# Attention stage of a four-stage block on one core: value bias as a one-row product, value eviction and query normalisation on ScalarE, normalisation statistics in other slots

## Chip, cores and metric

The kernel runs on one core of a Trainium2 chip. The metric is the device time of one execution in microseconds (us), from the first to the last instruction and what lies around them; lower is better. TensorE (PE) does matrix products and transposes, VectorE (DVE), ScalarE (ACT) and GpSimd (POOL) work element by element, SyncE (SP) issues the transfers.

## What is computed

The input x is 16 batches of 128 rows by 256 columns. Four residual parts follow one another: a recurrent mixing part, a gated feed-forward part, a cross attention and a mixture of experts. Only the cross attention and the last quarter of the feed-forward part, which runs beside its first batches, matter here:

```python
x = x + tanh(g_xattn[0]) * wkv(layernorm(x), ctx)
x = x + tanh(g_ffn[0])   * gated_ffn(layernorm(x))
x = x + tanh(g_xattn[1]) * attention(target=layernorm(x), source=ctx)   # 16 heads of 8
x = x + tanh(g_ffn[1])   * moe(layernorm(x))

# attention, for each batch:
q = Wq @ target + bq ;  k = Wk @ source + bk ;  v = Wv @ source + bv    # 128x256 each
amap = softmax(mask * (q.T @ k) / sqrt(8) - (1 - mask) * 1e6) * mask     # 256x256 per head
out  = amap @ v
```

layernorm(x) is (x - mean) / sqrt(var + 1e-5) over the 256 columns.

## The kernel before, in words

All four parts are written out by hand: each engine has its own list of instructions, and semaphores (names a_..., s_...) order them across engines. An engine works its list off strictly in order, so a wait holds up all that stands behind it.

The attention is a software pipeline over 16 batches. One batch is eight slots p = 0 to 7; batch b = 4g + k, with k the place in its group of four. The loop `turns` writes out group 0 (b = 0 to 3), runs groups 1 and 2 (b = 4 to 11) as a hardware loop and writes out the last group and one batch more. What is done in the eight slots of batch b belongs to several batches:

- the maxima of the scores of batch b+2. TensorE writes 16 score tiles (L782, 128x512 each as two products of 256 columns) by turns into two PSUM banks, and VectorE reduces each to row maxima (`dve_reduce`, L907). Two tiles, two reduces in each slot. I call these reduces R0 to R15. Score tile n+2 waits until reduce n has read its bank (`score_bank`, L796).
- the exponentials of batch b. TensorE writes the turned scores (L787) between the score products (`pe_both`), ScalarE takes the exponential of 128x1024 (`act_exp`, L982), and TensorE multiplies by the values (`pe_pv`, L853, two slots later).
- values of batch b+3: in slot 6 `pe_v` (L767) multiplies the context by Wv into the bank MISC, two products of 128x128. In slot 7, between R14 and R15, VectorE adds the bias row (bvb, a copy in all 128 partitions) and writes VF (`dve_vf`, L899). GpSimd makes VP of it (L1012).
- queries and keys of batch b+4. Statistics of x in slot 0 on VectorE, between the reduces (`dve_stats`, L876, L880, L883), the power -1/2 on GpSimd (`power_step`, L145), and in slot 1, between R2 and R3, VectorE writes the normalised tile Z3 (`dve_z3`, L893). TensorE makes the keys (L759) and then the queries (L763) of it in slot 1. ScalarE evicts both (`act_qk`, L958); masking, splitting and a trip through memory follow.
- the end of batch b-1: transposes on TensorE (L862 in slot 3, L869 in slot 5), the division and the addition to x on VectorE (L918 to L943).

One bank, MISC, holds by turns the values, the maxima turned (L841), keys and queries, and both transposes; each user waits until the one before has been evicted.

Ahead of slot 0 there is a prologue. The last quarter of the feed-forward part runs there on TensorE (L395, L431), and the projections and values of batches 0 to 2 stand between its products. VectorE does the feed-forward's element work (L409, L417), z3 and vf of these batches, and the reduces of batches 0 and 1.

## Time and profile before

| what | us |
|---|---|
| median of three runs | 611.96 |
| lowest and highest of them | 610.57, 614.04 |
| the profiled execution | 612.62 |
| span of that execution, first to last instruction | 610.9 |
| from one value product to the next, batches 1 to 11 | 14.39 |

The rows further down come from the profiled execution. "busy" is the time in which an engine works on an instruction; `[0.46 <-DVE MX L907]` behind a row says that the engine sat idle for 0.46 us before it and what ended that. A timeline row merges like instructions that follow each other: its first number is the start of the first one, its second the time until the end of the last. The end of a product lies later than the start of the next, since TensorE overlaps them, so on TensorE distances between starts are what counts. A product of 32-bit numbers shows as two MATMUL records, one for each of two passes; "x4" at L767 is therefore two products. The tile size ahead of the shape (60\*128, 64\*128, 128\*128, 128\*32) is the number of rows and columns of the array that the product uses.

### The profile page before, as it was taken

What the parts mean: (1) busy time and instruction counts of PE and PEld (TensorE: products, weight loads), DVE (VectorE), ACT (ScalarE), POOL (GpSimd) and SP (SyncE); (2) the same over time, 40 slices, a digit from 0 to 9 for tenths busy, and PEclk for the clock granted to TensorE, in tenths of its full rate; (3) what the DMA queues carried; (4) which work ended last, traced back from release to release, by engine and by line L of the source; (5) the groups of instructions that cost most, each with busy time, mean ns of one, the idle gap of its engine ahead of it and who ended that gap; (6) DMA issues with size and microseconds to landing.
All of it is one profiled execution on the core that took longest, in us unless ns stands there. A gap on an engine that the chain in (4) does not pass through costs nothing. (4 is left out here: it accounts for less than half of the span.)

```text
span 610.9 us, 10613 instructions
## 1 busy us (share of the span) xinstructions
PE 508.4 (83%) x3368; PEld 269.3 (44%) x3368; DVE 407.8 (67%) x881; ACT 228.1 (37%) x330; POOL 205.7 (34%) x350
## 2 busy tenths in 40 slices
PE   1159899999798879999999998989879999899960
PEld 1034554644453433333333433333333555788850
DVE  4978678687535778888888888886946333333224
ACT  1003012031032027777777777767611010132310
POOL 2514115132265134554545545531210710022220
PEclk9999999999999969999999999999979999999995
DMA  6602006673228334555555555530040220266518
GB/s 165 213 1 69 1 0 134 88 188 141 58 70 224 87 93 134 154 148 148 149 138 140 137 136 153 140 83 7 3 141 2 103 69 0 66 187 190 185 40 275
DMA packets 70882, 68.11 MB, mean 111 GB/s; under 512 B 9136, under 2 KB 63328, under 8 KB 70848
## 3 DMA queue, kind: packets, MB, share of 16 engines
q1 hardware_dynamic: 69312, 63.48, 38.9%
q0 software_dynamic: 1536, 4.20, 1.9%
q8 instruction: 18, 0.29, 0.2%
q14 instruction: 16, 0.13, 0.1%
HBM read 41.04 MB, written 26.62 MB: 111 GB/s over the span
## 5 line engine op out<-in xcount | busy, mean ns | idle before, releaser
L907 DVE TENSOR_REDUCE MX<-psum 128x2 f32<-128x512 f32 x256 | 166.7, 682 | 32.0 <-PE psum L782 32.0
L982 ACT ACTIVATE HP<-psum 128x1024 f32<-128x1024 f32 x128 | 129.9, 1023 | 56.5 <-PE psum L787 54.6
L782 PE MATMUL psum<-QKA 60*128 60x256 bf16 x512 | 86.3, 279 | 21.0 <-DVE MX L907 19.4
L395 PE MATMUL psum<-space_a,space_w 128*128 128x512 f32 (+1 forms) x192 | 89.8, 616 | 5.0 <-ACT space_a L384 2.9
L787 PE MATMUL psum<-QKA 60*128 60x256 bf16 x512 | 84.9, 276 | 0.2 <-ACT HP L982 0.2
L853 PE MATMUL psum<-HP,VP 128*32 128x256 f32 x1024 | 81.8, 393 | 0.3 <-issue 0.2
L782 PEld LDWEIGHTS psum<-QKA 60*128 60x128 bf16 x512 | 33.5, 95 | 82.0 <-DVE MX L907 68.1
L395 PEld LDWEIGHTS psum<-space_a,space_w 128*128 128x128 f32 (+1 forms) x192 | 34.4, 187 | 49.1 <-issue 39.1
L431 PE MATMUL psum<-space_w,HP 128*128 128x256 f32 x192 | 50.8, 402 | 2.2 <-DVE HP L417 2.2
L1629 PE MATMUL psum<-space_a,wsh 128*128 (+3 forms) x96 | 45.2, 622 | 1.1 <-PEq L1120 1.1
L1703 PE MATMUL psum<-XT,WE 128*128 128x256 f32 (+1 forms) x192 | 44.1, 380 | 1.6 <-ACT XT L1584 1.6
L1557 POOL DMA_INDIRECT combined<-OE,to_u x16 | 15.3, 959 | 87.4 <-ACT OE L1597 85.0
L431 PEld LDWEIGHTS psum<-space_w,HP 128*128 128x128 f32 x192 | 33.9, 193 | 16.5 <-issue 12.4
L1703 PEld LDWEIGHTS psum<-XT,WE 128*128 128x128 f32 (+1 forms) x192 | 34.2, 181 | 8.2 <-issue 1.1
L403 ACT ACTIVATE space_a<-psum,hgs 128x512 f32<-128x512 f32 (+1 forms) x24 | 16.5, 686 | 56.5 <-PE psum L395 56.5
L1012 POOL TENSOR_TENSOR VP<-VF,maskT 128x32 f32<-128x32 f32 x128 | 25.9, 239 | 28.0 <-DVE VF L899 14.8
L145 POOL TENSOR_TENSOR rstd<-veps,neghalf 128x1 f32<-128x1 f32 (+1 forms) x21 | 15.7, 748 | 54.5 <-DVE veps L127 44.4
L787 PEld LDWEIGHTS psum<-QKA 60*128 60x128 bf16 x512 | 31.1, 95 | 6.1 <-issue 2.9
L994 POOL TENSOR_TENSOR QK<-QK,MB 128x512 f32<-128x512 f32 x16 | 20.3, 1268 | 40.0 <-ACT QK L958 40.0
L409 DVE SCALAR_TENSOR_TENSOR space_a<-space_a,psum 128x512 f32<-128x512 f32 (+1 forms) x24 | 16.1, 672 | 24.1 <-ACT space_a L403 24.1
L853 PEld LDWEIGHTS psum<-HP,VP 128*32 128x32 f32 x1024 | 20.4, 108 | 26.5 <-issue 22.0
L1837 DVE SCALAR_TENSOR_TENSOR H1s<-THs,psum 128x256 f32<-128x256 f32 (+1 forms) x24 | 10.1, 420 | 28.8 <-ACT THs L1591 27.8
(167 smaller groups left out, 710.3 us busy)
## 6 DMA issues: line engine op xcount, KB each, us to landing
QKA<-stack_scr SPq DMA_DIRECT2D x32, 480.0 KB, 5.3
stack_scr<-PARTS SPq DMA_DIRECT2D x32, 192.0 KB, 2.1
WE<-in_W SPq DMA_DIRECT2D x16, 352.0 KB
stack_scr<-PARTS SPq DMA_DIRECT2D x32, 128.0 KB, 1.9
dispatched<-zeros SPq DMA_DIRECT2D x8, 257.0 KB, 3.6
XD<-dispatched SPq DMA_DIRECT2D x8, 257.0 KB, 3.0
X<-in_x SPq DMA_DIRECT2D x4, 512.0 KB, 3.6
CV<-in_ctx SPq DMA_DIRECT2D x4, 512.0 KB, 4.6
```

The source lines that it names most:

```text
L395: last = pe.matmul(bank[2 * (i % 2) + side][0:m, :], (gw, uw)[side][:, h, i * P:i * P + m], ZT[:, h, :], start=(h == 0), stop=(h == 1))
L403: act.activation(TH[0:m, i % 2, :], bank[2 * (i % 2)][0:m, :], ACT.Tanh, scale=hgs[0:m, i:i + 1]).then_inc(s_th, 1)
L431: last = pe.matmul(DB[t // 2][:, (t % 2) * C:(t % 2 + 1) * C], HP[0:m, i, t * P:(t + 1) * P], dw[0:m, i, :], start=(i == 0), stop=(i == NI ...
L782: return pe.matmul(SBK[n % 2][:, tt * T:(tt + 1) * T], QKA[rows, k, 0, h, tt * P:(tt + 1) * P], QKA[rows, k, 1, h, :], start=True, stop=True)
L787: return pe.matmul(TBK[st][:, j * T:(j + 1) * T], QKA[rows, k, 1, h, st * P:(st + 1) * P], QKA[rows, k, 0, h, :], start=True, stop=True)
L853: last = pe.matmul(PVB[32 * j:32 * j + 32, grp * T:(grp + 1) * T], VP[:, k, st, 4 * j + i, :], PT[:, i % 2, st, j, :], start=(i in (0, 3) ...
L907: dve.tensor_reduce(MX[:, par, head_of(n), :], SBK[n % 2][:, :].rearrange("p (a s) -> p a s", a=2), axis=AX.X, op=ALU.max).then_inc(a_red, 1)
L982: act.activation(PT[:, i % 2, st, :, :].rearrange("p j t -> p (j t)"), TBK[st], ACT.Exp)\
L994: pool.tensor_tensor(QK2, QK2, MB[:, k, :].unsqueeze(1).broadcast_to([P, 2, T]), ALU.mult).then_inc(a_masked, 1)
L1012: last = pool.tensor_tensor(dst, src, maskT[:, st, bass.ds(b, 1)].unsqueeze(2) .broadcast_to([P, 4, 8]), ALU.mult)
L1629: last = pe.matmul(bank[2 * i + side][0:m, :], (wsh1, wsh3)[side][:, h, i * P:i * P + m], ZT4[:, h, bass.ds(GT * g, GT)], start=(h == 0), ...
L1703: last = pe.matmul(bank[i][0:m, lo:lo + CAP], w[:, s, h, i * P:i * P + m], XT[:, s, h, :], start=(h == 0), stop=(h == 1))
```

## The change

1. Values: `pe_v` adds to each of its two products a second one that accumulates onto it: a stationary row of 128 ones (`one_row`, one partition) times one row of bvb. The eviction, now without an addition, moves to ScalarE (`act_vf`): in slot 7 behind the exponential.
2. Normalised query tile: ScalarE computes it as Identity(rstd * x + shift) (`act_z3`), with shift = -mean * rstd. VectorE makes negm = -mean beside veps (`dve_shift_terms`), GpSimd multiplies by rstd behind the power (`pool_shift`).
3. Other slots: for a batch at place 0 of its group, statistics and power stay in slot 0 of the batch four before it, and z3 stands in slot 1, ahead of that slot's exponential. For places 1 to 3 the statistics go to slots 5 and 6, the power and the shift to slot 6 and z3 to slot 7 of the batch five before it, so a whole slot 0 lies between z3 and the query product.
4. Prologue: z3 and vf of its batches stand in ScalarE's list.

```diff
@@ pe_v
                     for st in range(2):
-                        last = pe.matmul(MISC[:, st * P:(st + 1) * P], CX[:, k, st * P:(st + 1) * P], wv[:],
-                                         start=True, stop=True)
+                        pe.matmul(MISC[:, st * P:(st + 1) * P], CX[:, k, st * P:(st + 1) * P], wv[:], start=True, stop=False)
+                        last = pe.matmul(MISC[:, st * P:(st + 1) * P], one_row[:, :], bvb[0:1, :], start=False, stop=True)
                     last.then_inc(a_vps, 1)
@@
-                        dve.tensor_scalar(veps[:, 0:1], mv[:, 0:1, 1], EPS, None, ALU.add).then_inc(a_var, 1)
-
+                        dve_shift_terms(dve, 1)
+
+                def dve_shift_terms(dve, n):
+
+                    dve.tensor_scalar(veps[:, 0:n], mv[:, 0:n, 1], EPS, None, ALU.add).then_inc(a_var, 1)
+                    dve.tensor_scalar(negm[:, 0:n], mv[:, 0:n, 0], -1.0, None, ALU.mult).then_inc(a_var, 1)
@@
-                def dve_z3(dve, b):
+                def pool_shift(pool, n, nth):
+
+                    pool.wait_ge(a_var, 2 * nth)
+                    if later(nth - 1):
+                        pool.wait_ge(a_z3, nth + 2)
+                    pool.tensor_tensor(rstd[:, 0:n], veps[:, 0:n], neghalf[:, 0:n], ALU.pow).then_inc(a_rstd, 1)
+                    pool.wait_ge(a_rstd, nth)
+                    pool.tensor_tensor(shift[:, 0:n], negm[:, 0:n], rstd[:, 0:n], ALU.mult).then_inc(a_shift, 1)
+
+                def act_z3(act, b):
                     n = b if isinstance(b, int) and b < GB else 0
-                    dve.wait_ge(a_rstd, LN_COUNT(b))
+                    act.wait_ge(a_shift, LN_COUNT(b))
                     if later(b):
-                        dve.wait_ge(a_proj, b)
-                    dve.tensor_scalar(Z3[:], xb(b), mv[:, n, 0:1], rstd[:, n:n + 1], ALU.subtract, ALU.mult).then_inc(a_z3, 1)
-
-                def dve_vf(dve, b):
-                    dve.wait_ge(a_vps, b + 1)
+                        act.wait_ge(a_proj, b)
+                    act.activation(Z3[:], xb(b), ACT.Identity, bias=shift[:, n:n + 1], scale=rstd[:, n:n + 1]).then_inc(a_z3, 1)
+
+                def act_vf(act, b):
+                    act.wait_ge(a_vps, b + 1)
                     if later(b):
-                        dve.wait_ge(a_vp, b)
-                    dve.tensor_tensor(VF[:, :, :], MISC[:, 0:T].rearrange("p (s c) -> p s c", s=2),
-                                      bvb[:, :].unsqueeze(1).broadcast_to([P, 2, P]), ALU.add).then_inc(a_vf, 1)
+                        act.wait_ge(a_vp, b)
+                    act.activation(VF[:, :, :].rearrange("p s c -> p (s c)"), MISC[:, 0:T], ACT.Copy).then_inc(a_vf, 1)
@@ ScalarE's slot
+                            if p == 1 and k == 0 and there(b, AHEAD_Q):
+                                act_z3(act, b + AHEAD_Q)
...
+                            if p == 7 and there(b, AHEAD_V):
+                                act_vf(act, b + AHEAD_V)
+                            if p == 7 and k < GB - 1 and there(b, AHEAD_LN):
+                                act_z3(act, b + AHEAD_LN)
@@ GpSimd's slot
-                            if p == 0 and there(b, AHEAD_Q):
-                                power_step(pool, 1, a_var, a_rstd, LN_COUNT(b + AHEAD_Q))
+                            if p == 0 and k == 0 and there(b, AHEAD_Q):
+                                pool_shift(pool, 1, LN_COUNT(b + AHEAD_Q))
+                            if p == 6 and k < GB - 1 and there(b, AHEAD_LN):
+                                pool_shift(pool, 1, LN_COUNT(b + AHEAD_LN))
```

How this stands in the lists of the engines, first on TensorE. In slot 6 of a batch of the first group, the value products stand between the last attention product of the slot (L853) and the first score product of slot 7. Before:

```order
L787 MATMUL psum<-QKA 128x256
L853 MATMUL psum<-HP,VP 32x256 x4
L767 MATMUL psum<-wv,CX 128x128 x2
L782 MATMUL psum<-QKA 128x256
L787 MATMUL psum<-QKA 128x256
```

and in the changed kernel:

```order
L792 MATMUL psum<-QKA 128x256
L858 MATMUL psum<-HP,VP 32x256 x4
L772 MATMUL psum<-wv,CX 128x128
L773 MATMUL psum<-bvb,one_row 128x128
L772 MATMUL psum<-wv,CX 128x128
L773 MATMUL psum<-bvb,one_row 128x128
L787 MATMUL psum<-QKA 128x256
```

Two products have become four, and full ones (128 rows of the array) alternate with one-row ones.

VectorE from slot 5 of one batch to slot 3 of the next, in the first group (MX are the reduces, X<-X,psum is the addition of the batch before in slot 5). Before:

```order
L943 TENSOR_TENSOR X<-X,psum 128x256
L907 TENSOR_REDUCE MX<-psum 128x2 x3
L899 TENSOR_TENSOR VF<-psum,bvb 128x256
L907 TENSOR_REDUCE MX<-psum 128x2
L876 BN_STATS stats<-X 128x6
L907 TENSOR_REDUCE MX<-psum 128x2
L880 BN_AGGR mv<-stats 128x2
L907 TENSOR_REDUCE MX<-psum 128x2
L883 TENSOR_SCALAR veps<-mv 128x1
L907 TENSOR_REDUCE MX<-psum 128x2
L893 TENSOR_SCALAR Z<-X,mv,rstd 128x256
L907 TENSOR_REDUCE MX<-psum 128x2 x5
```

In the changed kernel the same stretch, from the statistics behind R11 on, reads:

```order
L881 BN_STATS stats<-X 128x6
L960 TENSOR_TENSOR X<-X,psum 128x256
L924 TENSOR_REDUCE MX<-psum 128x2
L885 BN_AGGR mv<-stats 128x2
L924 TENSOR_REDUCE MX<-psum 128x2
L892 TENSOR_SCALAR veps<-mv 128x1
L893 TENSOR_SCALAR negm<-mv 128x1
L924 TENSOR_REDUCE MX<-psum 128x2 x10
```

The ten reduces R14, R15, R0 to R7 now stand without anything between them, and the statistics have moved ahead of R14.

ScalarE from slot 5 to slot 1 (HP are the exponentials, NM the negated maxima, AV the eviction of the batch before). Before:

```order
L969 ACTIVATE PARTS<-QK 128x2x256
L982 ACTIVATE HP<-psum 128x1024 x3
L975 ACTIVATE NM<-psum 32x128
L987 ACTIVATE AV<-psum 128x512
L982 ACTIVATE HP<-psum 128x1024 x2
```

and in the changed kernel:

```order
L986 ACTIVATE PARTS<-QK 128x2x256
L999 ACTIVATE HP<-psum 128x1024 x2
L917 ACTIVATE VF<-psum 128x256
L911 ACTIVATE Z<-X,shift,rstd 128x256
L999 ACTIVATE HP<-psum 128x1024
L992 ACTIVATE NM<-psum 32x128
L1004 ACTIVATE AV<-psum 128x512
L999 ACTIVATE HP<-psum 128x1024 x2
```

The value eviction and the normalisation stand between the exponentials of slots 7 and 0.

## Rows read from the trace of the kernel before

**Rows 1.** Page, first part: busy us of an engine (share of the span), instructions.

```profile
PE 508.4 (83%) x3368; PEld 269.3 (44%) x3368; DVE 407.8 (67%) x881; ACT 228.1 (37%) x330; POOL 205.7 (34%) x350
```

**Rows 2.** Busy us by stretch: length, PE, PEld, DVE, ACT, POOL, clock, DMA share, GB/s.

```profile
275.00:315.00 40.00, 36.36 (x397) 14.98 (x393) 34.54 (x82) 28.80 (x39) 21.05 (x47) 1.00 0.52 135
```

**Rows 3.** Timeline of VectorE in one attention batch: start, us, line, operation, idle before.

```profile
279.48 0.69 DVE L907 TENSOR_REDUCE MX<-psum 128x2 f32<-128x512 f32 x1 [0.49 <-PE psum L782]
280.09 0.41 DVE L899 TENSOR_TENSOR VF<-psum,bvb 128x256 f32<-128x256 f32 x1
280.42 0.68 DVE L907 TENSOR_REDUCE MX<-psum 128x2 f32<-128x512 f32 x1
...
283.26 0.69 DVE L907 TENSOR_REDUCE MX<-psum 128x2 f32<-128x512 f32 x1 [0.52 <-PE psum L782]
283.87 0.57 DVE L893 TENSOR_SCALAR Z<-X,mv,rstd 128x256 f32 x1
...
293.87 0.69 DVE L907 TENSOR_REDUCE MX<-psum 128x2 f32<-128x512 f32 x1 [0.49 <-PE psum L782]
```

**Rows 4.** Timeline of TensorE in the same batch.

```profile
278.41 0.71 PE L767 MATMUL psum<-wv,CX 128*128 128x128 f32 x4
279.05 0.28 PE L782 MATMUL psum<-QKA 60*128 60x256 bf16 x1
...
281.16 0.28 PE L782 MATMUL psum<-QKA 60*128 60x256 bf16 x1 [0.46 <-DVE MX L907]
...
282.84 0.28 PE L782 MATMUL psum<-QKA 60*128 60x256 bf16 x1
...
283.38 0.70 PE L759 MATMUL psum<-CX,wk 128*128 128x256 f32 x2
284.49 0.70 PE L763 MATMUL psum<-Z,wq 128*128 128x256 f32 x2 [0.42 <-DVE Z L893]
285.12 0.28 PE L782 MATMUL psum<-QKA 60*128 60x256 bf16 x1
...
292.80 0.71 PE L767 MATMUL psum<-wv,CX 128*128 128x128 f32 x4
```

**Rows 5.** TensorE, feed-forward products of 128 and 64 rows, each row from its own start.

```profile
116.83 0.59 PE L431 MATMUL psum<-space_w,HP 128*128 128x256 f32 x2
...
117.05 0.79 PE L431 MATMUL psum<-space_w,HP 128*128 128x256 f32 x2
...
117.36 0.70 PE L431 MATMUL psum<-space_w,HP 64*128 64x256 f32 x2
...
117.68 0.79 PE L431 MATMUL psum<-space_w,HP 64*128 64x256 f32 x2
...
117.98 0.70 PE L431 MATMUL psum<-space_w,HP 128*128 128x256 f32 x2
```

**Rows 6.** Timeline of TensorE in the prologue.

```profile
174.32 0.61 PE L767 MATMUL psum<-wv,CX 128*128 128x128 f32 x4
174.76 3.60 PE L395 MATMUL psum<-space_a,space_w 128*128 128x512 f32 x8
178.20 0.59 PE L759 MATMUL psum<-CX,wk 128*128 128x256 f32 x2
178.63 0.59 PE L763 MATMUL psum<-Z,wq 128*128 128x256 f32 x2
```

**Rows 7.** Timelines of ScalarE and of GpSimd in the batch of rows 3.

```profile
279.74 1.02 ACT L982 ACTIVATE HP<-psum 128x1024 f32<-128x1024 f32 x1 [0.73 <-PE psum L787]
281.70 1.02 ACT L982 ACTIVATE HP<-psum 128x1024 f32<-128x1024 f32 x1 [0.94 <-PE psum L787]
...
280.58 1.62 POOL L1012 TENSOR_TENSOR VP<-VF,maskT 128x32 f32<-128x32 f32 x8 [1.48 <-DVE VF L899]
```

**Rows 8.** Groups by line and shape, 235 to 395 us: busy us, mean ns.

```profile
L958 ACT ACTIVATE QK<-psum,bqk 128x256 f32<-128x256 f32 x22 | 9.2, 473 | 0.0
...
L145 POOL TENSOR_TENSOR rstd<-veps,neghalf 128x1 f32<-128x1 f32 x11 | 6.0, 547 | 5.6 <-DVE veps L883 5.6
```

More of the change, by code:

```diff
@@ L76, in flamingo_kernel @@
         veps = sb("veps", [P, GB])
+        negm = sb("negm", [P, GB])
+        shift = sb("shift", [P, GB])
+        one_row = sb("one_row", [1, P])
         rstd = sb("rstd", [P, GB])
@@ L558, in _ @@
                     pool.memset(wgt[:, :, :], 0.0).then_inc(s_pool0, 1)
-                    pool.wait_ge(s_pool0, 10)
+                    pool.memset(one_row[:], 1.0).then_inc(s_pool0, 1)
+                    pool.wait_ge(s_pool0, 11)
                     pool.affine_select(out=ident[:], in_=ident[:], compare_op=ALU.not_equal, fill=1.0, base=0,
@@ L711, in flamingo_kernel @@
                 a_z3 = semp("a_z3")
+                a_shift = semp("a_shift")
                 a_proj = semp("a_proj")
@@ L741, in flamingo_kernel @@
                 PT = HP[:, :, :].rearrange("p (a s q) (r t) -> p a s (q r) t", a=2, s=2, r=2)
-                AHEAD_S, AHEAD_V, AHEAD_Q = 2, 3, 4
+                AHEAD_S, AHEAD_V, AHEAD_Q, AHEAD_LN = 2, 3, 4, 5
                 def xb(b):
@@ L1162, in _ @@
                         act_zt(act, G3)
+                        act_z3(act, 0)
                         act_qk(act, 0)
                         act_part(act, 0, 0)
+                        act_z3(act, 1)
                         for i in range(NI):
@@ L1171, in _ @@
                             if i in (1, 3):
+                                act_vf(act, i // 2)
                                 act_qk(act, i // 2 + 1)
+                                act_z3(act, i // 2 + 2)
+                        act_vf(act, 2)
                         act_nm(act, 0)
@@ L1196, in _ @@
                         pch = Chain(pool, a_pool)
-                        power_step(pool, GB, a_var, a_rstd, 1)
+                        pool_shift(pool, GB, 1)
                         for b in range(AHEAD_V):
@@ L1334, in _ @@
                         ch = Chain(dve, a_dve)
-                        last_of = layer_norm_stats(ch, xt_tile(0), GB)
-                        last_of.then_inc(a_var, 1)
+                        for b in range(GB):
+                            ch.do(dve.bn_stats(stats[:, b, :], xb(b)))
+                        ch.wait()
+                        for b in range(GB):
+                            ch.do(dve.bn_aggr(mv[:, b, :], stats[:, b, :]))
+                        ch.wait()
+                        dve_shift_terms(dve, GB)
                         dve.tensor_scalar(maskG[:, :, :], maskT[:, :, :], tg[:, 1:2], None, ALU.mult).then_inc(a_mg, 1)
-                        dve_z3(dve, 0)
                         def reduces(b, lo, hi):
@@ L1341, in reduces @@
                                 dve_reduce(dve, 0, b, h, PRO)
-                        dve_z3(dve, 1)
                         for i in range(NI):
@@ L1348, in _ @@
                             dve_h(dve, fch, G3, i)
-                            if i % 2 == 1:
-                                dve_vf(dve, i // 2)
-                            elif i > 0:
-                                dve_z3(dve, i // 2 + 1)
                         reduces(0, 4, 16)
@@ L1357, in _ @@
                         reduces(1, 12, 16)
+                        dve.wait_ge(a_z3, GB)
                         dve.wait_ge(a_mg, 1)
@@ L1361, in slot @@
                             b = GB * g + k
-                            if p == 0 and there(b, AHEAD_Q):
+                            if p == 0 and k == 0 and there(b, AHEAD_Q):
                                 dve_stats(dve, ch, b + AHEAD_Q, 0)
@@ L1365, in slot @@
                                 dve_reduce(dve, *at(g, k, AHEAD_S), 2 * p)
-                            if p == 0 and there(b, AHEAD_Q):
+                            if p == 0 and k == 0 and there(b, AHEAD_Q):
                                 dve_stats(dve, ch, b + AHEAD_Q, 1)
-                            if p == 1 and there(b, AHEAD_Q):
-                                dve_z3(dve, b + AHEAD_Q)
+                                dve_stats(dve, ch, b + AHEAD_Q, 2)
+                            if p == 6 and k < GB - 1 and there(b, AHEAD_LN):
+                                dve_stats(dve, ch, b + AHEAD_LN, 1)
                             if p == 4 and there(b, -1):
                                 dve_factors(dve, ch, b - 1)
-                            if p == 7 and there(b, AHEAD_V):
-                                dve_vf(dve, b + AHEAD_V)
                             if there(b, AHEAD_S):
                                 dve_reduce(dve, *at(g, k, AHEAD_S), 2 * p + 1)
-                            if p == 0 and there(b, AHEAD_Q):
-                                dve_stats(dve, ch, b + AHEAD_Q, 2)
+                            if p == 5 and k < GB - 1 and there(b, AHEAD_LN):
+                                dve_stats(dve, ch, b + AHEAD_LN, 0)
+                            if p == 6 and k < GB - 1 and there(b, AHEAD_LN):
+                                dve_stats(dve, ch, b + AHEAD_LN, 2)
                             if p == 3 and there(b, -1):
```

## The prediction, made before the changed kernel ran

> **What bounds the kernel now.** I read the page first, then one attention batch. Over the span TensorE is busy for 508.4 us and VectorE for 407.8, ScalarE and GpSimd for a third of it [rows 1], but that mixes stages. In a stretch of the attention loop TensorE works 36.4 of 40 us, VectorE 34.5, ScalarE 28.8 and GpSimd 21.1, at the full clock of 2.4 GHz (1.00) [rows 2]. Two engines near 90% that wait for each other: neither is free, and what counts is whose turn it is at a place. The reader is to see in the timelines that the turns alternate. VectorE waits 0.49 us for TensorE ahead of R14, the reduce at 279.48, and 0.52 ahead of R2 at 283.26 [rows 3]. TensorE waits 0.46 us for a reduce at 281.16 and 0.42 for the normalised tile Z at 284.49 [rows 4]. From R14 on, the path of a batch runs so:
>
> - R14, VF, R15 on VectorE, 279.48 to about 281.0, then TensorE's second half of slot 0 at 281.16
> - TensorE: attention product, turned maxima, attention product, the scores of slot 1 at 282.84, then R2 at 283.26
> - VectorE: R2, then Z at 283.87, and TensorE's query product at 284.49
> - TensorE: the scores of slot 2 at 285.12; from there by turns over slots 3 to 6, which the change leaves alone
> - TensorE: the value products at 292.80, slot 7's scores 0.64 later, R14 at 293.87.
>
> A batch takes 293.87 - 279.48 = 14.39 us, and the two value products are at 278.41 and 292.80, 14.39 apart [rows 3, 4]. So three of the edited pieces lie on the path: VF, Z, and the value products themselves. The statistics do not: they stand between reduces in slot 0, after which VectorE still waits 0.52 us.
>
> **VF off VectorE: a gain.** R15 starts 0.33 us after VF (280.42 against 280.09) [rows 3]. Without it R15, TensorE's half slot at 281.16 and all up to R2 come 0.33 earlier. On ScalarE the eviction finds room: between the exponentials at 279.74 and 281.70 it idles for 0.94 us [rows 7]. VF then is ready at about 281.1 rather than 280.5, and its reader VP on GpSimd, 1.62 us long, is needed batches later. 13 batches profit (1 to 13, the value products of slots 0 to 12): 13 x 0.33 = 4.3 us.
>
> **Z off VectorE and a slot earlier: a gain where it has gone from the path.** At places 1 to 3 the query product follows the keys at once. Keys at 283.38 and queries at 284.49, the next scores at 285.12: 1.74 us [rows 4]. The same two back to back in the prologue are 0.43 apart [rows 6], so two take 0.86, and with 0.20 for going into and out of full-size products (below) 1.06. That is 0.68 less. With VF a batch gains 1.01. It can just have it: R3 would start at 283.54 (R2 at 282.93 and 0.61 as now), and as R15 releases TensorE 0.74 after its start (280.42, 281.16), R3 would at 284.28; the second half of slot 2 asks for it at 284.11 + 0.22. Nine batches (1, 2, 3, 5, 6, 7, 9, 10, 11) gain 0.68 in this way: 6.1 us.
>
> On ScalarE Z stands behind VF. The nearest row is an eviction of the same size with a bias, 473 ns [rows 8]; two of these end about 0.1 us past the point where the next exponential could start, and that one has slack. Statistics in slots 5 and 6 (four small instructions) add some 0.6 us to VectorE ahead of R14, where it waits for the value products, 0.49 us now and 1.03 more by what follows. Were the added wait not there, as in rival A, they would cost about 0.1.
>
> At place 0 the chain stays inside the batch: the statistics, GpSimd's power (547 ns [rows 8]) and one more product of one column, then Z on ScalarE. GpSimd is held by VP, which now starts at about 281.15 instead of 280.58 [rows 7] and ends at 282.8; power to 283.35, shift to 283.6 (0.25, one of VP's eight pieces is 0.2), Z to 284.1, query product at 284.2 against 284.49. So batches 4 and 8 gain 0.29 instead of 0.33, batch 0 nothing. Bounds for the whole of Z: 6.1 us gained, or nothing at all if the chain is late everywhere. I take 6.0.
>
> **The one-row products: the loss.** They stand on the path, where VectorE waits for TensorE. Before, two products are 4 passes, and the next scores start 0.64 after the first [rows 4]; in the prologue, between products of the same tile size, 0.44 [rows 6], so 0.11 a pass. For 4 more passes the low end is 4 x 0.11 = 0.44 us.
>
> The trace has no one-row product. It has the nearest thing: the feed-forward's last block has 64 rows instead of 128 [rows 5]. Starts within one size are 0.22 apart (116.83, 117.05); into the smaller size 0.31 (117.36), its second pass 0.32 (117.68), and out of it 0.30 (117.98). Each change of size so costs 0.09 at the first pass and 0.10 at the second, 0.19 to 0.20 us. The new order full, one row, full, one row changes size at every product. In slot 6 the two changes at the ends exist already (0.64 - 0.44 = 0.20); four products then take 4 x (0.22 + 0.20) = 1.67 us, against 0.64. **I take 1.03 us more for each of 13 value steps: 13.4 us**, ends 0.44 and 1.03. I take the upper end since one row differs more from 128 than 64 does.
>
> On this step the Trainium skill speaks with two voices. "TensorE: Matmul & The Clock Gate", section "Step-by-step: what each phase is for", says that the weights of a next product are pulled ahead of the running one when row groups don't conflict or the background buffer is used, and that row count does not matter to a load. By this the added products would cost passes only, the low end. "TensorEngine Tiling (Array Packing)", section "Key Properties", says "Mode switching requires drain", which speaks against this order of products. The trace sides with the second for 64 rows (0.31 against 0.22 us); no row here shows it for one.
>
> **Prologue.** Four products between full-size ones change size four times: 8 x 0.11 + 4 x 0.20 = 1.67 against 0.44, 1.23 more. The first two value steps stand in a stretch without gaps on TensorE (the next feed-forward product starts at 174.76, right behind [rows 6]): 2.5 us. The third is followed by a wait for VectorE of over 2 us and is hidden. One Z (0.3) goes from VectorE ahead of the first reduces, and the same on ScalarE delays a tanh by 0.4. I take +2.5, ends 0 and 3.
>
> **Sum.** -4.3 - 6.0 + 13.4 + 2.5 = +5.6 us on a profiled 612.6, which is 0.7 above the median of 611.96; so **617.5 us** as a median, 0.9% slower. By batch: places 1 to 3 stay at about 14.4 us (-1.01 + 1.03), place 0 goes to about 15.1, batches 12 and 13 gain 0.33 and lose 1.03 in slot 6.
>
> **Rivals.**
>
> A. *The one-row products cost their passes only.* For it: weights are loaded during the product before wherever sizes are equal. Against: rows 5. Then 13 x 0.44 = 5.7, prologue 2 x 0.44 less 0.3 = 0.6: -10.3 + 6.3 = -4.0, **608 us, faster**. It decides at 0.79 us a step in the loop: below 10.3 / 13 = 0.79 the loop gains, above it loses. By the first page named this is what would happen.
>
> B. *A change of size costs one delay, not two* (0.1 each, so 0.74 a step): 9.6 - 10.3 + 1.4 = +0.7, **613 us**, no change. Nothing in rows 5 shows such a half price, but they are of another size.
>
> C. *Z comes late at all places*, because GpSimd's power and shift, or the exponential of slot 7, hold it past the key product. Then only VF's 4.3 is gained: +11.6, **623.5 us**. Against it: at places 1 to 3 a slot 0 of 2.3 us of TensorE time lies between.
>
> D. *The change doesn't do what it says*, VectorE still sets the pace: then the gains of 0.33 and 0.68 overlap and R3 is late. It has 0.04 us of slack by my reckoning, so some tenths a batch could be lost: 619 to 621, inside my range.
>
> **Chances.** Forecast with D 0.65, own range 614.5 to 621; A 0.12; B 0.13; C 0.10. To hold 8 in 10, the range takes the forecast, B in part and the lower part of C: 611.5 to 622. A measurement of this kernel can tell about 0.5% (3 us) from no change. Faster than 608.9: most of A and little else, 0.11. Within: B, the rest of A and the lower edge of the forecast, 0.20. Slower than 615.0: 0.69.
>
> **What would show it.** In the profile after: full-size and one-row products of the value step 0.4 us apart, 1.67 from its start to the next scores (A: 1.08, B: 1.4). TensorE waits for Z only at place 0, and there under 0.3 us less than now. VectorE's wait ahead of R14 grows from 0.49 to about 0.9 although most of the statistics have moved there, ahead of R2 it stays near 0.5. Value step to value step: 14.4 at places 1 to 3, about 15.1 at place 0. The clock stays at 1.00 in the loop. If the one-row products show starts 0.11 apart, the forecast is wrong in sign; if the wait for Z remains everywhere, it is C.

## The result, and the profile after

The changed kernel takes **618.0 us** (median of five executions, 614.54 to 619.33) beside 611.96 (610.57 to 615.77, five executions): ratio 1.0082, 95% interval 1.0054 to 1.0110. It is 0.8% slower; 617.5 was forecast.

The page's first part, the row that answers to [rows 1], and a stretch of the attention loop that answers to [rows 2]:

```profile
PE 518.9 (85%) x3432; PEld 278.7 (45%) x3432; DVE 396.8 (65%) x862; ACT 240.0 (39%) x362; POOL 208.1 (34%) x364
```

```profile
275.00:315.00 40.00, 37.97 (x400) 16.72 (x397) 31.81 (x78) 30.61 (x44) 20.70 (x49) 1.00 0.52 136
```

VectorE lost 2.7 of 40 us, ScalarE took over 1.8, and TensorE, which had 36.4, now works for 38.0. Work did leave VectorE, and it was TensorE that had no room for more.

**The value step**, timeline of TensorE at places 1 to 3, answering to [rows 4]. L772 is a full product, L773 the one-row product, L764 the keys, L768 the queries:

```profile
250.17 0.49 PE L772 MATMUL psum<-wv,CX 128*128 128x128 f32 x2
250.59 0.48 PE L773 MATMUL psum<-bvb,one_row 1*128 1x128 f32 x2
251.00 0.49 PE L772 MATMUL psum<-wv,CX 128*128 128x128 f32 x2
251.42 0.48 PE L773 MATMUL psum<-bvb,one_row 1*128 1x128 f32 x2
251.84 0.28 PE L787 MATMUL psum<-QKA 60*128 60x256 bf16 x1
...
255.83 0.70 PE L764 MATMUL psum<-CX,wk 128*128 128x256 f32 x2
256.36 0.59 PE L768 MATMUL psum<-Z,wq 128*128 128x256 f32 x2
256.89 0.28 PE L787 MATMUL psum<-QKA 60*128 60x256 bf16 x1
...
264.56 0.49 PE L772 MATMUL psum<-wv,CX 128*128 128x128 f32 x2
...
266.77 0.64 PE L858 MATMUL psum<-HP,VP 128*32 128x256 f32 x8
```

The starts lie 0.42, 0.41, 0.42 and 0.42 us apart, 1.67 from the first product to the next scores, where it was 0.64. The queries follow the keys at once (0.53 later, where it was 1.11) and no bracket stands behind them: TensorE no longer waits for Z at these places. From value step to value step it is 264.56 - 250.17 = 14.39 us, to the hundredth what it was. The attention products behind the value step (L858) start 266.77 - 264.56 = 2.21 us after it; a run below uses this.

**Place 0** (the batch whose Z is still made within the same batch): TensorE, then GpSimd, then ScalarE, answering to [rows 7].

```profile
285.92 0.70 PE L768 MATMUL psum<-Z,wq 128*128 128x256 f32 x2 [0.61 <-ACT Z L911]
```

```profile
282.68 1.62 POOL L1029 TENSOR_TENSOR VP<-VF,maskT 128x32 f32<-128x32 f32 x8 [3.03 <-ACT VF L917]
284.26 0.54 POOL L902 TENSOR_TENSOR rstd<-veps,neghalf 128x1 f32<-128x1 f32 x1
284.88 0.19 POOL L904 TENSOR_TENSOR shift<-negm,rstd 128x1 f32<-128x1 f32 x1
```

```profile
285.27 0.60 ACT L911 ACTIVATE Z<-X,shift,rstd 128x256 f32 x1 [0.47 <-POOL shift L904]
```

The power starts as soon as GpSimd is through with VP of the batch before, shift 0.62 later, Z 0.39 after that, and TensorE waits 0.61 us for Z (0.79 at the other place 0 of the loop), where it was 0.42. The two batches at place 0 in the loop take 15.27 and 15.45 us.

**VectorE's waits**, answering to [rows 3]. The first row is R14, R15, R0 and R1 at a place 1 to 3, the second R2 and R3 behind them, the third R14 and R15 ahead of place 0:

```profile
266.66 2.65 DVE L924 TENSOR_REDUCE MX<-psum 128x2 f32<-128x512 f32 x4 [1.00 <-PE psum L787]
270.11 1.29 DVE L924 TENSOR_REDUCE MX<-psum 128x2 f32<-128x512 f32 x2 [0.80 <-PE psum L787]
...
281.05 1.29 DVE L924 TENSOR_REDUCE MX<-psum 128x2 f32<-128x512 f32 x2 [1.51 <-PE psum L787]
```

What VectorE gave away it now spends waiting for TensorE: 1.00 and 1.51 us ahead of R14, where it was 0.49, and 0.80 ahead of R2, where it was 0.52 (at place 0, where the statistics still stand in slot 0, it is 0.30, at 284.50). From R14 to R2 it is 270.11 - 266.66 = 3.45 us, 0.33 less than the 3.78 of [rows 3].

**Prologue**, answering to [rows 6]: the first value step of the changed kernel, and the first feed-forward down product (L434, L431 before) behind the first two value steps, of the changed kernel and then of the kernel before.

```profile
172.46 0.38 PE L772 MATMUL psum<-wv,CX 128*128 128x128 f32 x2
...
174.01 3.70 PE L398 MATMUL psum<-space_a,space_w 128*128 128x512 f32 x8
...
195.97 1.19 PE L434 MATMUL psum<-space_w,HP 128*128 128x256 f32 x2 [1.15 <-DVE HP L420]
```

```profile
195.24 0.67 PE L431 MATMUL psum<-space_w,HP 128*128 128x256 f32 x2 [2.17 <-DVE HP L417]
```

The next feed-forward product starts 174.01 - 172.46 = 1.55 us after the value step, where it was 0.44. From the first value step to the second it is 9.39 us, where it was 8.18: 1.21 more.

**Where the profiled executions differ.** Spans are 610.9 and 612.8 us, 1.9 apart, while the medians are 6 apart. The marks, in TensorE's timeline of before and then of after (value step of batch 3, last attention products, first product of the mixture of experts):

```profile
235.25 0.71 PE L767 MATMUL psum<-wv,CX 128*128 128x128 f32 x4
...
444.04 1.83 PE L853 MATMUL psum<-HP,VP 128*32 128x256 f32 x24
...
450.37 6.12 PE L1629 MATMUL psum<-space_a,wsh 128*128 128x512 f32 x8 [1.08 <-PEq L1120]
```

```profile
235.78 0.49 PE L772 MATMUL psum<-wv,CX 128*128 128x128 f32 x2
...
447.94 1.83 PE L858 MATMUL psum<-HP,VP 128*32 128x256 f32 x24
...
453.72 3.67 PE L1660 MATMUL psum<-space_a,wsh 128*128 128x512 f32 x8 [0.78 <-PEq L1137]
```

| section | before | after | difference |
|---|---|---|---|
| start to first value step | 174.32 | 172.46 | -1.86 |
| first value step to first down product | 20.92 | 23.51 | +2.59 |
| to the value step of batch 3 | 40.01 | 39.81 | -0.20 |
| to the last attention products | 208.79 | 212.16 | +3.37 |
| to the mixture of experts | 6.33 | 5.78 | -0.55 |
| to the end of the span | 160.5 | 159.1 | -1.4 |

The second and the fourth section, where the edited value steps stand, are 6.0 us longer; the first, the fifth and the last section, which the change hardly touches, are together 3.8 shorter. In the first and behind the attention, the granted clock differs. Busy time by stretch of before, of after, and of a second profiled execution of the changed kernel with a span of 620.6 us (columns as in [rows 2]: length, five engines, clock, share and rate of the transfers):

```profile
164.00:171.00 7.00, 6.26 (x14) 3.15 (x14) 1.76 (x9) 1.58 (x4) 1.72 (x2) 0.76 0.49 147
...
448.00:475.00 27.00, 23.96 (x77) 10.95 (x78) 15.64 (x51) 3.29 (x6) 5.21 (x13) 0.87 0.27 89
```

```profile
164.00:171.00 7.00, 6.61 (x17) 3.25 (x18) 0.64 (x7) 3.06 (x7) 3.04 (x4) 1.00 0.41 133
...
448.00:475.00 27.00, 21.92 (x98) 9.12 (x96) 16.42 (x56) 4.92 (x8) 3.78 (x11) 1.00 0.24 81
```

```profile
164.00:171.00 7.00, 5.71 (x13) 3.27 (x14) 2.17 (x11) 1.79 (x3) 1.21 (x2) 0.53 0.51 151
```

In the first profiled execution of the changed kernel both stretches ran at the full clock; in the second, of the very same kernel, they had pieces at half clock (1.2 GHz; 0.53 and 0.87 in the two stretches), as before has. The first value step comes at 174.32 us in before, at 172.46 in the first profile after and at 177.03 in the second, in the order of these clocks. So the profiled execution, 614.54 us and the lowest of its five, is a lucky one. The attention loop stands at 1.00 in all three.

### The profile page after: what moved, and what is told of

Same layout as the page of the kernel before. It is cut to its first block and busy times, and to the rows that moved or that the text cites. A ratio compares the mean times of both kernels' runs of the same rounds, so it can differ in the third digit from the quotient of the medians.

```text
span 612.8 us, 10788 instructions
## 1 busy us (share of the span) xinstructions
PE 518.9 (85%) x3432; PEld 278.7 (45%) x3432; DVE 396.8 (65%) x862; ACT 240.0 (39%) x362; POOL 208.1 (34%) x364
## 5 line engine op out<-in xcount | busy, mean ns | idle before, releaser
L924 DVE TENSOR_REDUCE MX<-psum 128x2 f32<-128x512 f32 x256 | 164.7, 684 | 44.0 <-PE psum L787 43.2
L858 PE MATMUL psum<-HP,VP 128*32 128x256 f32 x1024 | 81.5, 391 | 0.3 <-issue 0.2
L434 PE MATMUL psum<-space_w,HP 128*128 128x256 f32 x192 | 51.0, 403 | 1.1 <-DVE HP L420 1.1
L1660 PE MATMUL psum<-space_a,wsh 128*128 (+3 forms) x96 | 42.8, 595 | 0.8 <-PEq L1137 0.8
L434 PEld LDWEIGHTS psum<-space_w,HP 128*128 128x128 f32 x192 | 33.9, 193 | 15.2 <-issue 11.2
L858 PEld LDWEIGHTS psum<-HP,VP 128*32 128x32 f32 x1024 | 20.4, 108 | 26.5 <-issue 22.2
L387 ACT ACTIVATE space_a<-psum 128x512 f32<-128x512 f32 x8 | 4.5, 595 | 66.3 <-PE psum L381 66.3
L1600 ACT ACTIVATE THs<-psum 128x512 f32<-128x512 f32 (+1 forms) x12 | 7.2, 596 | 55.9 <-PE psum L1660 55.9
```

What stands on the lines that cost most here:

```text
L434: last = pe.matmul(DB[t // 2][:, (t % 2) * C:(t % 2 + 1) * C], HP[0:m, i, t * P:(t + 1) * P], dw[0:m, i, :], start=(i == 0), stop=(i == NI ...
L858: last = pe.matmul(PVB[32 * j:32 * j + 32, grp * T:(grp + 1) * T], VP[:, k, st, 4 * j + i, :], PT[:, i % 2, st, j, :], start=(i in (0, 3) ...
L924: dve.tensor_reduce(MX[:, par, head_of(n), :], SBK[n % 2][:, :].rearrange("p (a s) -> p a s", a=2), axis=AX.X, op=ALU.max).then_inc(a_red, 1)
L1660: last = pe.matmul(bank[2 * i + side][0:m, :], (wsh1, wsh3)[side][:, h, i * P:i * P + m], ZT4[:, h, bass.ds(GT * g, GT)], start=(h == 0), ...
```

## The experiments

All ratios are to the kernel before, in the same session. "Place" times are distances between value steps in the profile, at places 1 to 3 and then at the two places 0 of the loop.

**The changed kernel again**, unchanged, as a measure for the others.

> The changed kernel as it is, once more, as the base of the other runs. My theory (a step of the value products 1.03 us longer in the loop and 1.23 in the prologue, less 10.3 us of VF and Z) puts the median 5 to 6 us above the kernel before, and the profile again shows 1.67 us for a value step, 14.39 us a batch at places 1 to 3 and 15.3 at place 0. The first profile had only 29.8 us at half clock against 41.6 in the one of before and was 2 us of span longer. If the time at half clock is an effect of the change, this profile shows about 30 us again and the span is again about 612.8; if it differs from execution to execution, it shows 33 to 45 and a span near 616.

Measured: 619.61 us (616.13 to 622.35), ratio 1.0092 [1.0056, 1.0128]; 14.39, and 15.28 and 15.45. The loop repeats to a hundredth, and the size of the loss is confirmed.

**Only the query part.** The values are made as before the change; normalisation, its slots and its engine are the changed kernel's.

```diff
@@ pe_v
-                        pe.matmul(MISC[...], CX[:, k, st * P:(st + 1) * P], wv[:], start=True, stop=False)
-                        last = pe.matmul(MISC[...], one_row[:, :], bvb[0:1, :], start=False, stop=True)
+                        last = pe.matmul(MISC[...], CX[:, k, st * P:(st + 1) * P], wv[:], start=True, stop=True)
@@ act_vf becomes dve_vf again, in VectorE's slot 7
+                    dve.tensor_tensor(VF[...], MISC[...], bvb[...], ALU.add).then_inc(a_vf, 1)
```

> Of the change only the part on the query: statistics in other slots, shift on GpSimd, Z on ScalarE. The value products have no row product and VF with its addition is on VectorE as before. My theory: the query product follows the keys at places 1 to 3, which gives 9 x 0.68 us; place 0 gains little or nothing. So 6 us below the kernel before (606), batches of 13.7 us at places 1 to 3. If the statistics in slots 5 and 6 cost something where the value step is short (R14 waits 0.49 us there): 13.8. Rival: VectorE sets the pace and the gain is given back; then within 2 us of before.

Measured: 606.90 us (603.48 to 608.22), ratio 0.9891 [0.9858, 0.9925]. Timeline of TensorE, value step, keys, queries, next value step:

```profile
249.48 0.71 PE L772 MATMUL psum<-wv,CX 128*128 128x128 f32 x4
254.45 0.70 PE L764 MATMUL psum<-CX,wk 128*128 128x256 f32 x2
254.99 0.59 PE L768 MATMUL psum<-Z,wq 128*128 128x256 f32 x2
263.19 0.71 PE L772 MATMUL psum<-wv,CX 128*128 128x128 f32 x4
```

263.19 - 249.48 = 13.71 against 14.39: the normalisation brings 0.69 us a batch at places 1 to 3, and at place 0 (14.39 and 14.18) nothing or 0.2. This half of the change is a gain.

**Only the value part**: the query part as before the change, the value part as changed.

```diff
@@ against the kernel before: pe_v, and vf in ScalarE's slot 7
+                        last = pe.matmul(MISC[...], one_row[:, :], bvb[0:1, :], start=False, stop=True)
+                            if p == 7 and there(b, AHEAD_V):
+                                act_vf(act, b + AHEAD_V)
```

> Of the change only the part on the values: the two row products and VF on ScalarE. Z and statistics stay on VectorE as before. My theory: +1.03 a step less 0.33 for VF, so a batch of 15.1 us in the loop, 12 or 13 x 0.7 = 9 us, and 2.5 in the prologue: 11.5 us above the kernel before (623.5). Rival (row products cost their passes only): +0.44 - 0.33 a batch, 2 to 3 us above.

Measured: 621.79 us (620.61 to 623.26), ratio 1.0143 [1.0114, 1.0172]; 14.92 in group 0, 14.97 in the loop. Both parts have their sign: one gains 1.1%, the other costs 1.4%. The batch came out 0.12 to 0.17 us shorter than expected, and TensorE's wait for Z is where it shows, 0.25 us in group 0 (0.30 to 0.32 in the loop) against 0.42 in [rows 4]:

```profile
245.06 0.70 PE L765 MATMUL psum<-Z,wq 128*128 128x256 f32 x2 [0.25 <-DVE Z L895]
```

Z takes VectorE 404 ns here in group 0 and 454 in the loop (means of its rows), and 570 in [rows 3]. What runs on GpSimd beside it differs between the two kernels, but no run isolates that.

**The size of the bias product.** Same number of products in the same order; only the rows of the stationary operand change. `one_row` becomes 128 partitions with ones in the first and zeros in the others, so each product has the full size and the same result.

```diff
-        one_row = sb("one_row", [1, P])
+        one_row = sb("one_row", [P, P])
...
-                    pool.memset(one_row[:], 1.0).then_inc(s_pool0, 1)
+                    pool.memset(one_row[:], 0.0).then_inc(s_pool0, 1)
+                    pool.memset(one_row[0:1, :], 1.0).then_inc(s_id, 1)
...
-                        last = pe.matmul(MISC[...], one_row[:, :], bvb[0:1, :], start=False, stop=True)
+                        last = pe.matmul(MISC[...], one_row[:, :], bvb[:, :], start=False, stop=True)
```

> The changed kernel with the bias product at full size: the stationary tile has 128 rows, of which the first holds ones and the others zeros, and the moving tile is bvb in all 128 partitions. Same number of products, columns and passes, no change of tile size. My theory: the passes of the value step are 0.11 us apart, a step takes 1.08 us instead of 1.67, so 13 x 0.59 = 7.7 us in the loop and 2 x 0.79 in the prologue less than the changed kernel: 608 to 609. Rival (the cost is that of two more products and their accumulation, whatever their size): no difference to the changed kernel.

Measured: 610.99 us (606.76 to 613.66), ratio 0.9952 [0.9923, 0.9981]; 13.82, and 14.70 and 14.88. Timeline of TensorE, the value step:

```profile
252.36 0.49 PE L773 MATMUL psum<-wv,CX 128*128 128x128 f32 x2
252.69 0.39 PE L774 MATMUL psum<-bvb,one_row 128*128 128x128 f32 x2
252.91 0.39 PE L773 MATMUL psum<-wv,CX 128*128 128x128 f32 x2
253.14 0.39 PE L774 MATMUL psum<-bvb,one_row 128*128 128x128 f32 x2
```

Starts are 0.33, 0.22 and 0.23 apart instead of 0.42. Multiplying 127 rows of zeros more is 0.58 us a step faster than leaving them out, and 8.6 us over the kernel (9.3 expected). This decides between the forecast and rival A: of the 1.03 us, 0.45 are the passes of the added products and 0.58 the changes of size, and without the changes the kernel would not have lost.

The weight loads (PEld) of the bias product show what differs, first in the changed kernel and then at full size:

```profile
250.59 0.29 PEld L773 LDWEIGHTS psum<-bvb,one_row 1*128 1x128 f32 x2
```

```profile
252.58 0.30 PEld L774 LDWEIGHTS psum<-bvb,one_row 128*128 128x128 f32 x2
```

At full size the load starts 0.11 us ahead of the product's first pass (252.69), beside the pass before it; the one-row load starts together with its product (250.59).

The same with 64 and with 96 rows:

> As the full-size run, but the bias product uses 64 rows of both tiles (row 0 ones, rows 1 to 63 zeros). My theory: a change of tile size as in the feed-forward's last block, so starts 0.42 us apart and a step of 1.67, as with one row. Rival (only the one-row form is dear): 0.22 apart and 1.08.

> The same with 96 rows. The experts' down products of 96 rows show no longer distance to those of 128 in the trace of before (starts 0.22 apart at 256 columns), so my theory expects no change of tile size here: starts 0.22 us apart, a step of 1.08, as at full size. If every difference in the row count costs, 0.42 and 1.67.

Measured, one execution each: 618.68 us and 14.29 with 64 rows, 611.00 us and 13.82 with 96 rows. With 64 rows, the first full product, the first pass of the last bias product, two score products beside it, and the attention products behind:

```profile
269.24 0.49 PE L773 MATMUL psum<-wv,CX 128*128 128x128 f32 x2
...
270.49 0.37 PE L774 MATMUL psum<-bvb,one_row 64*128 64x128 f32 x1
270.50 0.39 PE L793 MATMUL psum<-QKA 60*128 60x256 bf16 x2
...
271.34 0.64 PE L859 MATMUL psum<-HP,VP 128*32 128x256 f32 x8
```

96 rows behave as 128. 64 rows beside full products cost what one row costs (starts 0.42 apart), but the batch is 0.10 us shorter. The reason is at the end of the step: the 60-row scores of L793 start at 270.50, beside the last 64-row product, and those of L788 at 270.73; the attention products come 271.34 - 269.24 = 2.10 us after the first value product instead of 2.21. So the border lies between 64 and 96 rows, and 64-row and 60-row products share a size and even run side by side. One-row and 60-row products don't: in the changed kernel no score starts before 251.84, 0.42 after the start of the last one-row product.

**Fewer changes of size**: one one-row product over all 256 columns first, then the two full ones.

```diff
                 def pe_v(pe, k):
+                    pe.matmul(MISC[:, 0:T], one_row[:, :], bvb[0:1, :]... .broadcast_to([1, 2, P]), start=True, stop=False)
                     for st in range(2):
-                        pe.matmul(MISC[...], CX[:, k, st * P:(st + 1) * P], wv[:], start=True, stop=False)
-                        last = pe.matmul(MISC[...], one_row[:, :], bvb[0:1, :], start=False, stop=True)
+                        last = pe.matmul(MISC[...], CX[:, k, st * P:(st + 1) * P], wv[:], start=False, stop=(st == 1))
```

> The changed kernel with the bias laid down first, for both halves at once: one product of the row of ones with the bias row read twice (256 columns), then the two full value products, which accumulate onto it. The same columns of row products as before (2 x 128), but in a step one change of tile size inside instead of three, in the prologue two instead of four. My theory: a step of 1.27 to 1.3 us instead of 1.67, so 13 x 0.4 = 5.2 us in the loop and 0.8 in the prologue less than the changed kernel: about 6 us less in one session (613 where it has 619). Rival (each row product has a cost of its own, not the change of size): one product fewer of two, a step of about 1.2 to 1.25; the starts between the two full products decide: 0.22 us apart by my theory.

Measured: 611.41 us (609.64 to 613.36), ratio 0.9978 [0.9961, 0.9996]; 14.00, and 14.87 and 15.05.

```profile
250.39 0.69 PE L771 MATMUL psum<-bvb,one_row 1*128 1x256 f32 x2
251.01 0.71 PE L773 MATMUL psum<-wv,CX 128*128 128x128 f32 x4
251.65 0.28 PE L787 MATMUL psum<-QKA 60*128 60x256 bf16 x1
```

The same bias and the same one-row operand over the same columns, 1.26 us to the next scores instead of 1.67: two changes of size fewer, 0.2 us each. The order of the products alone is worth 0.4 us a batch.

**No bias product at all**: ScalarE copies the bare product, GpSimd adds the bias row to VF ahead of VP.

```diff
                 def pool_vp(pool, g, k):
                     pool.wait_ge(a_vf, b + 1)
+                    pool.tensor_tensor(VF[...], VF[...], bvb[...], ALU.add).then_inc(a_vb, 1)
+                    pool.wait_ge(a_vb, b + 1)
```

> The changed kernel without row products: the value products as before, VF by the plain eviction on ScalarE, and the bias added on GpSimd (one addition of 128x256 onto VF) ahead of VP. My theory: the step is 0.64 us again, which gives back 13 x 1.03 and 2.5 us; at place 0 the addition delays the power, the shift and Z by about 0.5 us, which costs 0.5 in two or three batches. 15 us below the changed kernel, 9 to 10 below the kernel before (603 to 604), batches of 13.4 us at places 1 to 3. The reserve that I reckoned there is 0.04 us, and the statistics ahead of R14 have no longer the long value step as cover: 13.4 to 13.5. Rival (VectorE sets the pace at this length): 13.7 as in the run with the query part alone, 606 to 607.

Measured: 605.91 us (605.79 to 606.89), ratio 0.9889 [0.9859, 0.9920]; 13.37 at places 1 to 3, but 15.07 and 15.26 at place 0, and one batch of 16.52, at a place 2. TensorE's query product at place 0:

```profile
282.33 0.70 PE L769 MATMUL psum<-Z,wq 128*128 128x256 f32 x2 [1.27 <-ACT Z L911]
```

The step saved is as large as expected, and two waits eat into it: for Z at place 0, and once, for 1.60 us at 307.81, for the maxima that come back from memory. Place 0 takes 1.70 us more than places 1 to 3, where it was 0.88 in the changed kernel: the addition on GpSimd costs 0.8 us there, and 0.5 was expected.

**Power and shift ahead of VP at place 0**, in the last kernel and in the changed one. If VP holds up GpSimd, turning the two round should help.

```diff
                             if p == 0 and k == 0 and there(b, AHEAD_Q):
                                 pool_shift(pool, 1, LN_COUNT(b + AHEAD_Q))
+                            if p == 0 and k == 0 and not (isinstance(b, int) and b == 0) and there(b, 2):
+                                pool_vp(pool, *at(g, k, 2))
...
-                            if p == 7 and there(b, AHEAD_V):
+                            if p == 7 and k < GB - 1 and there(b, AHEAD_V):
                                 pool_vp(pool, *at(g, k, AHEAD_V))
```

> The kernel with the bias added on GpSimd, and in it GpSimd's power and shift for the batch at place 0 put ahead of the bias addition and VP of the batch before it (8 instructions plus 1, 2.35 us in its profile), instead of behind them. My reading: at place 0 these 2.35 us hold the power, which started at 280.65 although its terms were ready at 279.27; the power moves to about 279.3, Z to about 280.55 (then held by ScalarE's AV, which ends there) instead of 281.68, and TensorE's wait for Z of 1.27 us falls to about 0.15. Batches at place 0 go from 15.07 and 15.26 to about 14.0, places 1 to 3 stay at 13.4: 605.9 - 2.3 = 603.6 us. The other reading: the wait at place 0 is set by the statistics of VectorE and the length of the chain itself; then it stays above 1 us, place 0 at 15.1, and the time at 606.

> The changed kernel with the same one move: at place 0 GpSimd's power and shift ahead of VP of the batch before. In the changed kernel's profile the power started at 284.26 behind VP, its terms were ready at 283.59; it moves 0.6 us forward, Z on ScalarE from 285.27 to about 284.8 (held by AV), TensorE's wait of 0.61 us for Z falls to about 0.15. Batches at place 0: 15.27 and 15.45 become about 14.8 both, places 1 to 3 stay at 14.39, and the time at 617 to 618.5 us, about 1 us less than the changed kernel, which one run can't tell. If the chain alone sets Z, place 0 stays at 15.3 to 15.45.

Measured, with the bias on GpSimd: **602.54 us** (601.77 to 606.45), ratio 0.9817 [0.9794, 0.9839], the fastest of all; place 0 takes 13.84 and 13.76. GpSimd, then ScalarE, then TensorE at place 0:

```profile
279.39 0.56 POOL L902 TENSOR_TENSOR rstd<-veps,neghalf 128x1 f32<-128x1 f32 x1 [3.09 <-DVE negm L893]
```

```profile
279.84 0.60 ACT L1004 ACTIVATE AV<-psum 128x512 f32<-128x512 f32 x1
280.41 0.60 ACT L911 ACTIVATE Z<-X,shift,rstd 128x256 f32 x1
```

```profile
280.24 0.70 PE L765 MATMUL psum<-CX,wk 128*128 128x256 f32 x2
281.06 0.70 PE L769 MATMUL psum<-Z,wq 128*128 128x256 f32 x2
```

The power now waits for its terms (negm) instead of for GpSimd. The bracket for Z is gone, but Z still holds the queries a little. They follow the keys after 0.82 us instead of 0.53, right at the end of Z (281.01), and Z now stands behind the eviction AV on ScalarE. In the changed kernel the same move gives 14.76 and 14.77 instead of 15.27 and 15.45, with the queries 0.81 behind the keys, and 618.2 us in its one execution. So VP on GpSimd held place 0 up in both, by 0.5 to 0.7 us in the changed kernel and by 1.2 to 1.5 with the bias on GpSimd; of the 0.4 to 0.5 us by which place 0 is still longer than places 1 to 3, some 0.3 is Z behind AV.

One slow batch is left in the fastest kernel, 16.44 us, at the same place 2. TensorE waits 1.51 us for the maxima there, and this stretch follows, TensorE busy throughout at 1.2 GHz:

```profile
308.40:311.60 3.20, 3.20 (x18) 1.62 (x12) 1.29 (x2) 1.81 (x4) 1.75 (x5) 0.50 0.36 92
```

The two together would account for the 3.07 us over 13.37: 1.51 of wait, and about 1.6 for 3.2 us at half the clock. Why this one transfer comes late, and why at this batch alone, stays open.

**All kernels by one sum.** From the query part alone (13.70 as the mean of its batches) everything else follows at places 1 to 3:

| kernel | value step | VF | worked out | measured |
|---|---|---|---|---|
| query part only | 0.64 | VectorE | | 13.70 |
| bias on GpSimd | 0.64 | ScalarE | 13.70 - 0.33 = 13.37 | 13.37 |
| full-size bias product | 1.09 | ScalarE | 13.37 + 0.45 = 13.82 | 13.82 |
| one-row product first | 1.26 | ScalarE | 13.37 + 0.62 = 13.99 | 14.00 |
| 64-row bias product | 1.56 | ScalarE | 13.37 + 0.92 = 14.29 | 14.29 |
| changed kernel | 1.67 | ScalarE | 13.37 + 1.03 = 14.40 | 14.39 |

The value step is the time from its first product to the next scores; with 64 rows, where scores start beside it, it is 1.67 less the 0.11 by which the attention products come sooner. TensorE's value step goes into the batch one for one, which is what a step on the path must do. With the query part still as before, the sum misses: 14.39 - 0.33 + 1.03 = 15.09 against 14.92 and 14.97.

## Why the prediction was right, step by step

- **What bounds the kernel.** Right. The path was read as turns between TensorE and VectorE with VF, Z and the value products on it, and each of the three moved the batch time by its own size (table above).
- **VF off VectorE, 0.33 a batch.** Right: 13.70 with VF on VectorE, 13.37 without. ScalarE found room for it; its copy takes 0.38 us.
- **Z off VectorE and earlier, 0.68 at places 1 to 3.** Right: 14.39 became 13.70 or 13.71, 0.69. The estimate for keys and queries together, made from rows of the prologue, was 1.06 us; in the trace after it is 256.89 - 255.83 = 1.06.
- **The value step, 1.03 more.** Right, to the hundredth: 1.67. The pair of facts that carried it was in [rows 5]: 0.09 and 0.10 us at each change between 128 and 64 rows. That one row costs as much as 64 was a choice of the upper end, and the runs with one, 64, 96 and 128 rows bear it out. They do not bear out the reason given for it, that one row differs more from 128 than 64 does: beside full products one row and 64 rows cost the same, and 96 rows nothing. Rival A (1.08 a step) is what the kernel with the full-size bias product shows, at 1.09: the mechanism is real, but only for products of one size. Rival B's half price appears nowhere. On the two pages of the Trainium skill: "TensorEngine Tiling (Array Packing)", section "Key Properties", has the rule that decided here, that a change of tiling mode drains the engine; by it, the trace agrees (0.42 against 0.22 us a product). What "TensorE: Matmul & The Clock Gate", section "Step-by-step: what each phase is for", says of weights that are pulled ahead is seen only within a size: the load 0.11 us ahead of its product at full size, and together with it where the size changes.
- **Place 0.** The mis-sized term. The prediction had Z on ScalarE start at 283.6, at the end of shift, and hand over at 284.1, and gain 0.29 us a batch. Against the 14.39 of before, the loop's places 0 take 15.27 and 15.45 where 15.1 was forecast. Three prices were too low: Z takes 0.60 us on ScalarE and not 0.47 (the nearest row had one operand per partition, Z has two), it starts 0.39 after shift, and shift starts 0.62 after the power. Over the two batches of the loop that is 0.5 us, so it hardly moved the sum. The sign named for it failed, too: TensorE's wait for Z at place 0 was to fall from 0.42, and it grew to 0.61 and 0.79. VP's hold on GpSimd was named in the prediction, and its weight was shown by the last two runs; that AV on ScalarE holds Z next was not in it.
- **VectorE's wait ahead of R14.** Forecast about 0.9, measured 1.00; ahead of place 0, where no statistics stand in slots 5 and 6, 1.51. That the wait ahead of R2 would stay near 0.5 was a miss without a price: it is 0.80, since the statistics that left slot 0 left idle time behind (0.30 at place 0, where they stayed).
- **Prologue, 2.5.** 2.59 from the first value step to the first down product, and the step itself is right (1.21 more from the first value step to the second, 1.23 forecast). That the whole agrees so well is in part luck: for the same section the kernel with the query part alone takes 21.33 us, 0.41 more than before, and the one with the value part alone 198.59 - 174.26 = 24.33, 3.41 more. The parts don't add up to 2.59; ahead of the third value step TensorE waits for a reduce, 0.58 us in before, 0.74 in the changed kernel and 1.56 with the value part alone. The forecast left this wait as it was.
- **The sum.** +5.6 forecast. The second and the fourth section of the trace give +6.0, the two ratios of 1.0082 and 1.0092 give 5.0 and 5.6 us (intervals 3.3 to 6.7 and 3.4 to 7.8). The profiled pair alone, +1.9, would have spoken against it; that the clock makes up the rest is read from the sections and windows, no run held the clock fixed.
- **Rivals C and D.** The kernel without the query part is nearly what C describes, 621.8 us: worse by 2 us than the changed kernel in the medians, and by 4.2 in the two traces from the value step of batch 3 to the last one, not by 6. Places 0 are shorter in it (14.92 and 14.96 against 15.28 and 15.45), and the other batches only 0.5 to 0.6 longer instead of 0.68, by TensorE's shorter wait for Z. Where the rest of the difference between 4.2 and 2 went is not shown. D did not appear: no reduce is late at places 1 to 3.

## What to carry to other kernels

Before a small product is added to save work elsewhere, look at the number of rows of its neighbours: a product of one or of 64 rows between full ones cost 0.2 us at every change of size here, padding it with zeros to the full size took that away, and putting it first saved two changes of four. Move work off an engine that shares the path only if the engine that gets the replacement isn't the other half of the path; an engine with idle time beside the path (GpSimd here) took the same bias without lengthening the batches of places 1 to 3 (13.37), and cost little at place 0 once its order put the urgent small instructions ahead of the long ones. Judge by distances between like marks within a stretch at the full clock, and test each half of a change alone: here a gain of 1.1% was hidden behind a loss of 1.4%.

## What was not expected of the hardware

- 127 rows of zeros more make a product cheaper among its full-size neighbours: 0.22 us instead of 0.42. The border lies between 64 and 96 rows. A change between 64 and 60 rows costs nothing, and products of these two sizes start 0.01 us apart, side by side; between one row and 60 rows the scores start 0.42 us after the last one-row product, 0.21 after its second pass, as at a change of size.
- An ACTIVATE of 128x256 takes 378 ns as a plain copy, 473 with one operand per partition and 600 with two. That is 95 ns for the first and 127 for the second, if nothing else counts; the first two read PSUM and the third reads SBUF, and no run takes this apart.
- Half-clock stretches come and go between executions of one kernel. The same changed kernel had spans of 612.8 and 620.6 us, with the attention loop equal to a hundredth of a microsecond. A single profiled execution can so hide, or feign, a difference of 1%.
- A wait of 1.5 us for a transfer in a loop that otherwise keeps TensorE busy was followed by over 3 us at 1.2 GHz in both profiled executions that had it (two kernels, bias on GpSimd), which by the estimate above doubled its price.
